# Second feed-forward moved to the lower half of the arena, with a ring of three blocks and a newly planned walk

## The reference, cut to what matters

```python
logits = einsum('bsh,he->bse', x, router_w) + router_b + load_balancer
rw, sel = top_k(logits, 2); rw = softmax(rw)
e0 = silu(x @ sw_w1) * (x @ sw_w3) @ sw_w2
sym = ((x @ me_eq_w + me_eq_b) @ me_wv + me_bv) @ me_wo + me_bo
e1 = gelu(sym @ me_c1w + me_c1b) @ me_c2w + me_c2b
syn = x @ ce_syn_w + ce_syn_b
h2 = layer_norm(syn + (syn @ ce_wv + ce_bv) @ ce_wo + ce_bo, ce_n1g, ce_n1b)
ff = relu(h2 @ ce_f1w + ce_f1b) @ ce_f2w + ce_f2b
e2 = layer_norm(h2 + ff, ce_n2g, ce_n2b) @ ce_gen_w + ce_gen_b
e3 = gelu(x @ ml_w1 + ml_b1) @ ml_w2 + ml_b2
out = sum over the two chosen experts of rw * expert
```

## Time and profile before

| | us |
|---|---|
| median of 3 runs (lowest, highest) | 1068.76 (1068.43, 1069.16) |
| the profiled execution | 1070.11 |
| its span | 1068.3 |
| TensorE busy | 991.4 |
| VectorE, ScalarE, GpSimd busy | 738.2, 660.8, 332.5 |
| mean granted TensorE clock | 0.961 |

### The profile page before, as it was taken

The page is one execution under the profiler, slowest core; times in us unless marked ns, Lnnn a source line. Parts: engine busy times, 40 slices in busy tenths (PEclk is TensorE's granted clock), DMA queues, the critical chain, the costliest instruction groups (busy, mean ns, idle before and its releaser), DMA issues.

```text
span 1068.3 us, 21784 instructions
## 1 busy us (share of the span) xinstructions
PE 991.4 (93%) x7902; PEld 653.3 (61%) x7902; DVE 738.2 (69%) x2788; ACT 660.8 (62%) x1497; POOL 332.5 (31%) x728
## 2 busy tenths in 40 slices
PE   6998999999988899999999988799978999999996
PEld 4887565554446656577777745364336666576675
DVE  2656789798978857576453756787896876875523
ACT  3688988885542335668788675536433225687873
POOL 2875343524202022235423322042122012451321
PEclk9999999999986999999999999899977899999999
DMA  9300001032341100010000000204241110000001
GB/s 319 135 1 2 0 2 50 1 90 53 67 91 41 24 18 11 11 40 1 30 11 11 11 10 11 60 1 111 64 98 38 21 32 11 11 11 1 11 1 30
DMA packets 71642, 41.23 MB, mean 39 GB/s; under 512 B 52208, under 2 KB 63856, under 8 KB 71280
## 3 DMA queue, kind: packets, MB, share of 16 engines
...
## 4 chain that ended last, share of the span: by engine, by line
PE 58%; DVE 24%; ACT 9%; DMA 3%; issue 3%; POOL 2%; SPq 1%; ACTq 0%; POOLq 0%; DVEq 0%
PE psum L1040 7%; PE psum L933 5%; PE psum L509 5%; DVE sol_t L1513 5%; DVE pool L1508 5%; PE psum L1030 3%; DVE pool L1457 3%; PE psum L1024 3%; PE psum L1026 2%; PE psum L802 2%; PE psum L863 2%; PE psum L518 2%; PE psum L776 2%; PE psum L774 2%; ACT pool L1737 2%
## 5 line engine op out<-in xcount | busy, mean ns | idle before, releaser
L1723 ACT ACTIVATE pool<-psum 128x512 f32<-128x512 f32 x144 | 83.7, 598 | 83.2 <-PE psum L863 33.1
L1737 ACT ACTIVATE pool<-pool,small 128x128 f32<-128x128 f32 x224 | 92.1, 484 | 57.4 <-POOL small L2103 57.3
L509 PE MATMUL psum<-sb_const,pool 128*128 128x128 f32 x672 | 101.5, 286 | 8.8 <-ACT pool L1737 4.4
L863 PE MATMUL psum<-pool,firw 128*32 128x512 f32 (+7 forms) x960 | 105.4, 588 | 3.7 <-POOL pool L2178 3.7
L509 PEld LDWEIGHTS psum<-sb_const,pool 128*128 128x128 f32 x672 | 80.8, 147 | 45.7 <-issue 19.8
L2098 POOL TENSOR_SCALAR small<-small 128x4 f32<-128x4 f32 x88 | 23.4, 265 | 268.3 <-DVE small L1111 266.3
L2101 POOL TENSOR_TENSOR small<-small,minus_half 128x4 f32<-128x4 f32 x88 | 92.3, 1049 | 7.3
L933 PE MATMUL psum<-pool,sb_l1a 128*128 128x512 f32 x192 | 89.1, 617 | 0.7 <-ACT pool L1723 0.7
L1328 DVE TENSOR_TENSOR pool<-pool,psum 128x512 f32<-128x512 f32 x80 | 52.7, 681 | 51.8 <-ACT pool L2007 29.7
L1040 PE MATMUL psum<-sb_l1f,pool 128*128 128x128 f32 x640 | 80.7, 278 | 0.0
L1040 PEld LDWEIGHTS psum<-sb_l1f,pool 128*128 128x128 f32 x640 | 75.7, 192 | 5.5 <-issue 3.3
...
## 6 DMA issues: line engine op xcount, KB each, us to landing
...
```

Source lines behind the costliest of these rows:

```text
L509: m = e.transpose(f.ap[:, part(b)], src[:, part(b)], ident)
L863: m = e.matmul(b4(f.ap)[32 * c:32 * c + 32, :, 4 * kg:], firw[:, col, :], vsh[:, c, :, 0:P - 4 * kg], start=n == 0, stop=n == len(kgs) - 1)
L1723: e.activation(slot(g, i), f.ap, ACT.Copy).then_inc(f.emptied, 1)
L1737: m = e.activation(dst[:, part(b)], src[:, part(b)], ACT.Identity, bias=v["nm"][:, b:b + 1], scale=v["r"][:, b:b + 1])
```

## The change

1. The `g_b` steps go to slots 2, 3 and 7 of the lower half. 2. The ring of `g_h` has three blocks, slots 4 to 6. 3. `g_b2` makes only one copy of the normalized tile; the bias f2b, which its second activation added, goes into the bank of `g_b4` by `with_bias(f, 0)`, and the setup step `s_g3` puts f2b into the split rows. 4. `branch_read` becomes `upper_read`: the loads of group g + 4 wait for `b_wo` of group g. 5. The wait for the output of group g goes from `f_lt` to the places where group g + 4 first writes its upper half (`upper_half`, called in `b_sh`, `b_q` and `b_k2`). 6. In `small`, `idx2` and shifted offsets keep the second mixture's scratch apart from that of the next group's. 7. The walk is written anew: the same 1766 steps in another order. From the walk only the lines that the later text speaks of are shown.

```diff
 ORDER (old lines, each with "..." where lines lie between)
-b_q2/3 b_x.6-15/2 b_u.1/0 b_xo/1 b_vT/3 b_fir.0-1/3 b_p.1/0 b_fir.2-3/3 b_u.0/1 b_u.2/0 b_x.16-19/2 b_p.0/1 b_x.20/2
...
-b_x.52-55/3 b_p.1/2 b_oT/1 b_x.56-58/3 b_u.2/2 b_x.59-61/3 b_xo/3 b_w/0 b_mx.0/0 b_oF/1 b_mx.1-3/0 b_ac/0 b_ms/0
-b_p.2/2 b_at/2 b_on/0 b_u.0/3 b_r.0/1 b_p.0/3 y_v/0 b_nF/0 b_u.3/2 b_u.1/3 b_wo/0 b_na/0 b_r.1/1 b_p.1/3 y_tr/0 y_k/0
...
-b_k/4 f_lg/5 b_vT/4 f_lg/6 f_lt/5 f_lt/6 b_qs/4 b_q2/4 f_mu/5 f_mu/6 f_hid.0/5 b_ks/4 b_k2/4 g_na/3 g_out/3
-f_hid.1-2/5 b_fir.0-1/4 b_ss/4 f_cnt/5 f_cnt/6 f_hid.5/7 f_gl/5 f_gl/6 b_qn/4 f_hid.3-5/5 b_gg/4 f_gw/5 f_e.0-4/5
...
-b_u.2/4 b_x.26-35/6 b_p.0/5 b_qn/7 b_gg/7 b_kk/7 b_p.2/4 b_u.1/5 b_x.36-38/6 b_u.3/4 b_at/4 b_us/4 b_p.1/5 b_x.39-43/6
-b_ag/7 b_sol/7 b_x.0/7 b_o/4 b_x.44-50/6 b_u.2/5 b_oT/4 b_x.51-57/6 b_p.2/5 b_x.58/6 b_oF/4 b_x.59-61/6 b_xo/6 b_at/5
...
-g_h.5-6/7 g_e2/7 g_na/5 g_out/5 g_d.3-4/7 g_na/6 g_out/6 g_h.7/7 g_d.5/7 g_e0/7 g_h.8/7 g_e1/7 g_h.9/7 g_d.6-9/7
-g_e3/7 g_st/7 g_na/7 g_out/7
 (new lines)
+b_q2/3 b_u.0/0 b_kk/2 b_ag/2 b_sol/2 b_p.0/0 b_x.29-30/1 b_vT/3 b_x.31-61/1 b_x.0-1/2 b_k/3 b_xo/1 b_u.1/0 b_fir.0-2/3
+b_p.1/0 b_x.2-7/2 b_fir.3/3 b_u.2/0 b_x.8-14/2 b_ks/3 b_x.15-20/2 b_u.0/1 b_p.2/0 b_x.21-25/2 b_p.0/1 b_at/0 b_k2/3
...
+b_xo/3 b_w/0 b_mx.0-3/0 b_u.2/2 b_p.2/2 b_oF/1 b_ac/0 b_ms/0 b_at/2 b_on/0 b_u.0/3 b_r.0/1 b_p.0/3 y_k/0 b_nF/0
...
+f_lg/5 f_lg/6 f_lt/5 b_qs/4 b_q2/4 f_lt/6 g_na/3 f_mu/5 b_k2/4 f_mu/6 f_hid.0/5 b_ss/4 b_fir.0-1/4 f_hid.1/5 g_out/3
...
+b_x.20-21/6 b_u.2/4 b_p.0/5 b_qn/7 b_gg/7 b_kk/7 b_ag/7 b_sol/7 b_x.22-23/6 b_p.2/4 b_u.1/5 b_at/4 b_u.3/4 b_us/4
...
+g_h.9/6 g_h.9/5 g_d.8-9/6 g_d.8-9/5 g_e3/5 g_b7/5 g_e3/6 g_e0/7 g_b7/6 g_d.6/7 g_e2/5 g_st/5 g_e2/6 g_st/6 g_e1/7
+g_d.7/7 g_h.8-9/7 g_b7/7 g_d.8/7 g_e2/7 g_na/5 g_d.9/7 g_e3/7 g_st/7 g_na/6 g_out/5 g_out/6 g_na/7 g_out/7
@@ program @@
-    def branch_read(own, g):
-        f = fill("g_b7", g)
+    def upper_read(own, g):
+        f = fill("b_wo", g)
         own.wait_ge(f.filled, f.n)
     def upper_half(own, g):
         if g + NA in EARLY:
             own.wait_ge(sem(f"parked{g % NA}"), 16)
+        elif g >= NA:
+            own.wait_ge(sem(f"out{g % NA}"), 16)
@@ sync: a_load and f_load @@
-                branch_read(o, g - NA)
+                upper_read(o, g - NA)
@@ tensor @@
-                m = e.matmul(f.ap[:, part(b)], slot(g, 4 + k % 4)[:, part(b)], weight,
+                m = e.matmul(f.ap[:, part(b)], slot(g, 4 + k % 3)[:, part(b)], weight,
         def g_b4(g, k):
             f = begin("g_b4", g)
+            with_bias(f, 0)
             for b in range(GB):
-                opened(f, slot(g, 10), b, b == 0)
+                opened(f, slot(g, 3), b, False)
@@ vector: f_lt @@
-            if g >= NA:
-                o.wait_ge(sem(f"out{g % NA}"), 16)
@@ scalar @@
         def g_b2(g, k):
-            e.activation(slot(g, 9), f.ap, ACT.Identity, bias=wt("l1f", "n1b"), scale=wt("l1f", "n1g"))
-            e.activation(slot(g, 10), f.ap, ACT.Identity, bias=nfb[:, 0:1], scale=wt("l1f", "n1g")).then_inc(f.emptied, 1)
+            e.activation(slot(g, 3), f.ap, ACT.Identity, bias=wt("l1f", "n1b"), scale=wt("l1f", "n1g")).then_inc(f.emptied, 1)
```

More of the change, by code:

```diff
@@ L49 @@
[L49 to L58, removed]
@@ L69 @@
[L69 to L78, removed]
@@ L79 @@
[L79 to L88, removed]
@@ L94 @@
[L94 to L97, removed]
-b_x.4-9/5 b_vT/7 b_qs/7 b_x.10-14/5 b_kk/6 b_u.0/4 b_x.15-25/5 b_ks/7 b_k2/7 b_x.26-50/5 b_ag/6 b_x.51-52/5 b_p.0/4
@@ new lines @@
+b_tr/1 c_pT/7 f_hid.0-2/2 c_hF/6 c_nb/3 c_pv/7 b_k/1 f_cnt/2 f_tr/3 c_w1/6 f_hid.0/3 f_hid.3-4/2 c_ft/6 c_na/7 b_q/1
+c_hF/7 f_gl/2 b_v/1 b_qs/1 c_fa/6 f_lg/3 b_fir.3/0 f_lt/3 b_vs/1 b_sh/1 c_w1/7 b_ks/1 b_kk/0 b_ag/0 b_sol/0 f_gw/2
+f_hid.5/2 f_hid.1/3 b_ez/1 b_q2/1 f_hid.2/3 f_e.0-3/2 b_k2/1 f_hid.3/3 b_ss/1 f_e.4-5/2 f_mu/3 f_d.0-1/2 c_ft/7 b_vT/1
+f_d.2-5/2 f_out/2 c_nb/6 b_fir.0/1 c_park/6 f_cnt/3 c_fa/7 f_gl/3 f_na/2 b_x.0-1/0 b_fir.1-2/1 b_tr/2 f_hid.4/3
+b_x.2-3/0 b_k/2 f_hid.5/3 c_nb/7 c_park/7 b_qn/1 b_v/2 b_gg/1 b_vs/2 b_sh/2 f_gw/3 b_ez/2 b_fir.3/1 b_x.4-15/0
@@ new lines @@
+b_w/1 b_p.2/3 b_at/3 y_ex/0 y_pT/0 b_oF/2 b_mx.0-3/1 y_pv/0 y_na/0 b_ac/1 b_ms/1 b_u.3/3 b_r.0-1/2 b_us/3 g_tr/0 y_v/1
+b_o/3 b_on/1 g_b0/0 g_lg/0 b_oT/3 b_nF/1 a_load/4 b_lg/2 g_wd/0 b_wo/1 g_h.0-1/0 b_oF/3 g_b1/0 b_na/1 b_lt/2 b_w/2
+b_mx.0-3/2 b_r.0/3 b_ac/2 b_ms/2 b_r.1/3 y_tr/1 g_h.2/0 y_k/1 b_on/2 y_q/1 g_d.0/0 g_h.3/0 b_nF/2 y_sc/1 b_lg/3
+g_d.1-3/0 g_e0/0 y_ex/1 g_b2/0 y_pT/1 b_wo/2 a_y/4 b_lt/3 b_w/3 y_pv/1 g_b3.0-1/0 b_mx.0/3 b_na/2 g_b4/0 y_tr/2
+g_h.4-6/0 a_load/5 y_na/1 y_v/2 b_mx.1-2/3 g_b5/0 b_mx.3/3 b_ac/3 b_ms/3 y_k/2 g_tr/1 g_d.4/0 g_h.7/0 g_d.5/0 g_e1/0
@@ new lines @@
+a_na/5 g_e1/3 f_hid.0/6 c_nb/4 g_d.7/3 g_st/2 g_b5/3 x_tr/5 f_hid.1/6 f_tr/4 x_q/5 f_lg/4 g_out/0 g_h.9/3 g_b6/3
+x_sc/5 x_v/5 f_lt/4 x_ex/5 g_d.8/3 f_mu/4 f_hid.0-2/4 g_d.9/3 g_e3/3 x_pT/5 g_b7/3 x_pv/5 f_cnt/4 f_hid.3/4 x_na/5
+g_e2/3 f_hid.4-5/4 x_hF/5 f_gl/4 c_q/5 c_sc/5 c_ex/5 f_hid.0/7 f_hid.2/6 f_gw/4 f_hid.1-2/7 f_e.0-5/4 g_st/3 g_na/1
+c_pT/5 f_d.0-1/4 g_out/1 c_pv/5 c_na/5 f_d.2-5/4 f_out/4 f_hid.3/6 c_hF/5 f_hid.3/7 f_na/4 c_w1/5 f_hid.4/6 b_tr/4
+c_ft/5 b_v/4 c_fa/5 g_na/2 b_vs/4 b_sh/4 f_hid.5/6 b_k/4 c_nb/5 b_q/4 f_hid.4/7 g_out/2 b_ez/4 f_tr/5 b_ks/4 b_vT/4
@@ new lines @@
+b_k2/6 b_qs/6 b_q2/6 f_d.2-4/7 b_fir.0-2/5 b_vT/6 b_x.2-5/4 b_ss/5 b_qn/5 b_gg/5 f_d.5/7 f_out/7 b_ss/6 b_ez/6
+b_x.6-12/4 b_fir.3/5 f_na/7 b_kk/5 b_ag/5 b_sol/5 b_x.13-50/4 b_fir.0-1/6 b_x.51-61/4 b_xo/4 b_fir.2/6 b_qn/6 b_tr/7
+b_gg/6 b_v/7 b_x.0/5 b_vs/7 b_x.1-2/5 b_q/7 b_k/7 b_qs/7 b_sh/7 b_fir.3/6 b_ks/7 b_ez/7 b_x.3-5/5 b_kk/6 b_ag/6
+b_sol/6 b_x.6-35/5 b_u.0/4 b_x.36-50/5 b_x.0-1/6 b_k2/7 b_x.51/5 b_x.2/6 b_x.52/5 b_x.3/6 b_x.53/5 b_x.4/6 b_q2/7
+b_p.0/4 b_x.54-57/5 b_ss/7 b_x.58-61/5 b_xo/5 b_vT/7 b_fir.0-2/7 b_u.1/4 b_p.1/4 b_fir.3/7 b_x.5-19/6 b_u.0/5
```

145 lines of the change are left out of this document (82 added, 63 removed).

## The result

The changed kernel took 1075.97 us (median of 5, 1074.23 to 1079.83) against 1068.43 us for the kernel before on the same chip: a ratio of 1.0083, 95% interval 1.0057 to 1.0109. In a second comparison, with 12 executions, it was 1.0057 (1.0034 to 1.0080). So it is 6 to 9 us slower, where -3.5 us had been forecast. The profiled execution took 1075.97 us around a span of 1074.1 us, 5.8 us more than the span before.

What follows compares the result with a forecast made beforehand. TensorE, busy 991.4 of 1068.3 us, was taken as the bound, with VectorE setting the pace in the solves. Terms 2.6 - 1.5 - 3.3 - 1.0 - 1.1 + 0.8 = -3.5 us gave 1065.3 us from 1068.8; range 1057 to 1075.

Steps and rivals of the forecast that it cites:

- (1): Bias in `g_b4`: four more bf16 matmuls in each of 8 groups, in full TensorE stretches, +2.6 us.
- (2): ScalarE: eight activations fewer (-6.2 us) against five more table loads (+6.4), under a full TensorE: 0.
- (3): Earlier input loads and moved output wait: no matmul waits for a load, none is held, 0.
- (8): Setup's extra copy and dropped VectorE sum, new slots, ring of three that the walk respects by order: 0.
- (4): Hollow, 614 to 694 us: wait at `b_ss/4` moves to `f_cnt/6`, -1.5 us, bounds 0 and -6.8.
- Rival C: Much faster: earlier `f_tr/6` and `/7` fill half of the hollow, 6.7 us more, 1058.6 us; chance 0.10.
- (5): Fourth solve: the wait of `b_x.0/7` for the matrix read-back goes whole, -3.3 us, bounds 0 and -3.3.
- (6): Two solution read-backs, DMA waits at `b_u.0/1` and `b_u.0/3`: -1.0 and -1.1 us, bounds 0 and -3.7.
- rival B: No difference: waits go elsewhere, the fourth solve's returning as a wait for `b_at/4`, 1068.6 us; chance 0.20.
- grown `b_p` waits: Sign that the prediction is wrong: `b_u` or `b_p` waits grow in the solving stretches; no size given.
- (7): Tail: VectorE becomes the last, behind TensorE, with its final expert sums, +0.8 us, bounds 0 and +3.
- Rival A: Slower: TensorE waits for ScalarE from 400 to 614 us; loads, bias and tail add 6.0, 1074.8 us; chance 0.30.

Runs made afterwards that it cites:

- e3: Kernel before with the bias edit alone (four bias matmuls in `g_b4`, one activation fewer in `g_b2`), old walk: 1.0016.
- e2: Changed kernel without the four bias matmuls of `g_b4` in each group: 1.0049 of the kernel before.
- e17: Kernel before with the bias edit, ring of four, six `g_h` of groups 0 to 3 moved behind their `g_d`: executed once, 1078.5 us, not compared.
- e7: Changed code under the old walk, groups 4 to 7 keeping a ring of four, so only six `g_h` of groups 0 to 3 moved: 1.0055.
- e1: Changed code under the old walk, with only the 18 `g_h` that a ring of three forbids moved down: 1.0075.
- e8: Code of the kernel before, old walk up to step 1085, new walk behind (second delta rule and end): 1.0006.
- e11: Changed kernel with one step moved, `b_ks/7` from ahead of `b_kk/6` to behind `b_u.0/4`: 1.0109 of the kernel before.
- e12: Code of the kernel before, old walk but steps 1085 to 1541 in the new order with `b_ks/7` moved: 0.9976.
- e18: Code of the kernel before, old walk but steps 1085 to 1541 in the new order, `b_ks/7` not moved, a repeat: 0.9981.
- e6: Code of the kernel before, new walk for the first 256 steps, old walk behind: 1.0028.

## Why the prediction was wrong, by its steps

The step that failed is the one ahead of all the terms: "The same work lies ahead of each of these points, so the full stretches can't shrink; the change lives on single waits." That the same work lies ahead holds at the four common places, and the rest doesn't follow. With the same steps, the full stretches grew: the middle by 3.3 us and the last by 2.6, of which the bias is at most 0.8 and 1.3. And I counted the single waits that the new order would close without those that it would open. The forecast's gains (-1.5, -3.3 and -2.1 us) did not arrive, and two terms that it put at nothing, the order that a ring of three forces and the start, did.

(1) The bias, +2.6: right in mechanism and size where TensorE is full. The changed kernel has 128 such matmuls; the sixteen more in the last stretch take 1.3 us by the starts of the rows, and e3 measures 1.4 there. In the middle, under the old walk, a part of it fell into a wait: +0.8 by the table. Together +2.2. Under the new walk e2 gives 1.2 in the last stretch and nothing in the middle, where the waits take all of it.

(2) ScalarE, 0: the loads came as counted, 85 in fourteen groups instead of 80 in thirteen. From 400 to 614 us TensorE idles 3.0 us instead of 1.8, so what ScalarE can have cost there is at most 1.2 us; no run takes the five loads out alone. The timeline of ScalarE in the changed kernel has an activation 1.29 us behind the start of its table load, and no idle time ahead of the load, which leaves no room for a drain:

```profile
678.62 1.28 ACT L1872 ACT_TABLE_LOAD   x1
679.91 0.31 ACT L1872 ACTIVATE small<-small 128x128 f32<-128x128 f32 x1
```

By this row the trace disagrees with the Trainium skill (ScalarE: Activation LUTs, section What ACT_TABLE_LOAD costs), which charges a drain as well.

(3) and (8) The ring and the loads, 0: the loads' new condition and the moved output wait cost nothing under the old walk (e17 has neither and takes as long as e7); the loads' earlier places were not tested alone. The ring of three "which the walk respects by order" is the term that I left out: respecting it costs 2.8 us in the middle (e17 against e3) and 5.3 us in the last stretch (e1 against e7), if the old walk is bent as little as possible. Of the 5.3 us 3.8 are idle time of TensorE, in waits for VectorE and ScalarE that name neither the ring nor `g_d` (1.3, 0.9, 0.7, 0.4 and 0.4 us in e1, none in e7). The new walk pays about as much in the middle, 2.5 us beyond the bias as e3 has it and 3.4 us by e2, which has none, and in the last stretch 1.3 us by e3 and 1.9 by e8. In the last stretch nothing asks for a ring of three, since no load follows. That the new walk's price in the middle has the same cause wasn't separated: under the old code its loads would wait for a `g_b7` that stands behind them.

(4) The hollow, -1.5: wrong. The wait moved to `f_cnt/6` as said, 1.37 us, but at `f_tr/5`, a step that I hadn't looked at, 5.65 us stand instead of 2.48, and the three large waits add to 9.3 us as before. In the whole middle the waits that name ScalarE grow from 6.5 to 13.8 us, and those that name VectorE and GpSimd fall from 8.6 to 1.9. Rival C, the filled hollow, has nothing in its favour.

(5) and (6) Solves and read-backs, -5.4: the waits went as foretold or further, and the gain was not there. The whole second delta rule gives 1.0 us with a spread of 1.7 and 1.1. This is rival B in another place: VectorE no longer waits for the DMA, but for `b_p`, which TensorE brings late behind a filter of 6.33 us; grown `b_p` waits were named as a sign of being wrong. e11 and e12 show that this stretch hands a closed wait on. In the first delta rule the DMA wait of 1.99 us at `b_u.0/1` is gone and the one at `b_u.0/3` is down from 1.74 to 0.62 us, while a new one of 1.33 us stands at 290.59 us. Over all profiles TensorE idles 13.5 us there with the new order and 15.5 with the old, but its granted clock is at the lower level (0.5 of full speed, 1.2 GHz) for 43.1 us instead of 33.5 (from the trace's clock records), and the stretch is no shorter (+1.0, spread 2.8). Which of the two gave and which took stays open, since they move together under the old order too (e18: 41.0 us at the lower level and 13.0 idle; before: 30.7 and 17.3). Case C's remark that a closed wait there gives more than its length is not borne out.

(7) The tail, +0.8: right in kind, VectorE last and without idle time, but +0.2 in size.

The start, counted as 0 in step (8), costs 2.1 us by the profiles and 0.0029 (3.1 us) by the mean of the three differences. I had read its setup steps and not its order. TensorE idles 21.6 us up to place 256 with the new order (mean of seven profiles) and 19.4 with the old (thirteen), and is busy for 169.8 us in both: on average the whole difference is idle time. Some of the new waits are small ones for ScalarE: in e6 two of 0.69 us at 21.08 and 23.32 us, one of 0.35 at 29.96 and one of 0.74 at 59.52, where e8 with the old order has none. The clock adds scatter and takes another course under the new start (last section).

Rival A gave 1074.8 us, near the result, by another way. In the full stretch from 400 to 614 us the named waits are for ScalarE, but they grew only from 1.5 to 2.8 us, where A asked for 2.6 us more; the rest of its price was the bias and the tail. The time came from three places of 2 to 3 us each, so its nearness is luck.
